# Low one-hots from the read banks on ScalarE instead of a compare on VectorE

## What is computed

```python
item_emb = concat(table_i1[item[:, 0]], table_i2[item[:, 1]], table_i3[item[:, 2]])        # 96 wide
ub = concat(table_i1[rec_his[:, :, 0]], table_i2[rec_his[:, :, 1]], table_i3[rec_his[:, :, 2]])
h = concat(q, ub, q - ub, q * ub) @ w_att1.T + b_att1       # q: item_emb at each position
score = (h @ w_att2.T + b_att2)[..., 0]                     # linear in ub, given q
score = where(rec_his[:, :, 0] == 0, 0.0, score)
browse = einsum('bl,ble->be', score, ub)
x = dice(concat(item_emb, browse, user_emb) @ w1.T + b1)
x = dice(x @ w2.T + b2)
out = sigmoid(x @ w3.T + b3)
```

## Time and profile before

| | |
|---|---|
| three timed runs | 1511.55, 1507.39, 1504.20 us |
| span of the profiled execution | 1506.3 us (its time outside the span is not given) |
| VectorE, TensorE, GpSimd, ScalarE busy | 93%, 86%, 79%, 50% |
| mean TensorE clock granted | 0.957 of full |
| main loop | about 50 to 1450 us |

### The profile page before, as it was taken

The page is one execution under the profiler, slowest core; times in us unless marked ns, Lnnn a source line. Parts: engine busy times, 40 slices in busy tenths (PEclk is TensorE's granted clock), DMA queues, the critical chain, the costliest instruction groups (busy, mean ns, idle before and its releaser), DMA issues.

```text
span 1506.3 us, 66273 instructions
## 1 busy us (share of the span) xinstructions
PE 1299.2 (86%) x27007; PEld 1186.0 (79%) x27007; DVE 1405.9 (93%) x1397; ACT 758.1 (50%) x1729; POOL 1188.4 (79%) x1671
## 2 busy tenths in 40 slices
PE   5688989889898988889898998989899898988864
PEld 4577878888887988788788888878888887888761
DVE  6699999999999999899999999999999999999945
ACT  5554455555445555454555554454555545452217
POOL 3588788888888888788888888888888888888830
PEclk8899999999999999999999999999999999999966
DMA  3566676666667666666766666666676666565820
GB/s 51 111 137 127 127 143 133 141 144 141 124 137 143 130 146 140 127 133 133 143 131 142 146 141 134 130 137 132 143 143 140 141 132 138 131 149 133 153 54 1
DMA packets 517508, 194.38 MB, mean 129 GB/s; under 512 B 485445, under 2 KB 493237, under 8 KB 517245
## 3 DMA queue, kind: packets, MB, share of 16 engines
q1 hardware_dynamic: 499654, 162.61, 53.5%
q10 hardware_dynamic: 15448, 26.51, 6.7%
q0 software_dynamic: 2144, 1.36, 0.8%
HBM read 8.45 MB, written 1.44 MB: 7 GB/s over the span
## 4 chain that ended last, share of the span: by engine, by line
POOL 72%; issue 15%; PE 3%; DVE 3%; POOLq 3%; ACT 2%; DMA 1%; ACTq 1%; SPq 0%; DVEq 0%
POOL score L439 24%; POOL score_r L448 14%; POOL score L444 11%; POOL parts L449 9%; POOL parts L452 6%; POOL item_rows L417 4%; POOL parts L445 3%; POOL user_rows L425 2%; DVE score_j L1026 1%; DVE onehot_lo L1012 1%; ACT scores_b L775 1%; PE sel L727 1%; DMA hiT<-onehot_hi 1%; POOLq L437 1%; POOLq L443 1%
## 5 line engine op out<-in xcount | busy, mean ns | idle before, releaser
L560 PE MATMUL wsum_ps<-scaled_lo,onehot_hi 100*128 100x75 bf16 x12288 | 535.0, 201 | 81.5 <-DVE scaled_lo L1038 80.2
L543 PEld LDWEIGHTS sel<-scoretab,hiT 128*128 128x128 bf16 x12288 | 495.8, 99 | 121.6 <-DMA hiT<-onehot_hi 59.2
L543 PE MATMUL sel<-scoretab,hiT 128*128 128x75 bf16 x12288 | 534.5, 201 | 63.1 <-DMA hiT<-onehot_hi 43.9
L1038 DVE TENSOR_TENSOR scaled_lo<-onehot_lo,parts 100x3744 bf16<-100x3744 bf16 x256 | 539.0, 2105 | 34.4 <-POOL parts L452 26.4
L560 PEld LDWEIGHTS wsum_ps<-scaled_lo,onehot_hi 100*128 100x128 bf16 x12288 | 486.1, 99 | 106.3 <-DVE scaled_lo L1038 101.7
L439 POOL TENSOR_TENSOR score<-score_j 100x16 f32<-100x16 f32 x256 | 386.6, 1510 | 156.6 <-DVE score_j L1026 155.7
L768 ACT ACTIVATE wsum_ring<-wsum_ps 128x300 f32<-128x300 f32 x512 | 215.5, 421 | 525.7 <-PE wsum_ps L560 497.2
L1026 DVE TENSOR_REDUCE score_j<-sel 100x24 f32<-100x600 f32 x512 | 395.5, 772 | 21.0 <-PE sel L543 21.0
L994 DVE TENSOR_TENSOR onehot_hi<-digits,iota_hi 100x1920 bf16<-100x1920 bf16 x256 | 296.1, 1157 | 3.4 <-PE wsum_ps L560 3.3
L775 ACT ACTIVATE scores_b<-acc 128x512 bf16<-128x512 f32 (+1 forms) x318 | 255.4, 803 | 50.0 <-issue 22.7
L448 POOL TENSOR_TENSOR score_r<-score,parts 100x16 f32<-100x16 f32 x256 | 207.3, 810 | 20.0
(11 more groups left out here) (168 smaller groups left out, 724.0 us busy)
## 6 DMA issues: line engine op xcount, KB each, us to landing
scoretab<-scores_b SPq DMA_DIRECT2D x384, 93.8 KB
weightsum<-wsum_ring ACTq DMA_DIRECT2D x128, 125.0 KB
weightsum<-wsum_ring ACTq DMA_DIRECT2D x64, 150.0 KB
raw<-in_r_rec_his_dram SPq DMA_DIRECT2D x32, 150.0 KB
hiT<-onehot_hi SPq DMA_TRANSPOSE x256, 3.8
x_rows<-x_tile SPq DMA_DIRECT2D x14, 100.0 KB
scores_b<-x_rows SPq DMA_DIRECT2D x1, 1400.0 KB
item_rows<-in_L_rec_table_i_dram,ids_now POOLq DMA_INDIRECT x51
```

Source lines behind the costliest of these rows:

```text
L543: mm = pe.matmul(sel[:, 2 * (s % 2) + q, (c % 4) * W:(c % 4 + 1) * W] .rearrange("p (j v) -> p j v", j=NF), hiT[0:HJ, s // 2 % 4, g * POSP ...
L560: mm = pe.matmul(wsum_ps[:, s % 2, b * W:(b + 1) * W].rearrange("p (j v) -> p j v", j=NF), hi_columns(ring_slot(n), g), scaled_lo[:, n % 2 ...
L1038: ins = dve.tensor_tensor(scaled_lo[:, n % 2, :, :, :].rearrange("p q i (u d) -> p (q i) u d", d=2), onehot_lo[:, n % 2, :, :, :].rearrang ...
```

## The change

The low compare on VectorE goes. ScalarE makes the low one-hots, 8 half histories at a time, out of the banks that `read_scores` filled: `relu(1 + x / 2^100)` is 1 in the matching column and 0 in all others. It does so after VectorE's pick of the same slot and behind `copy_sums` in its own order; `read_scores` two slots later waits for it too. `onehot_lo` has four buffers instead of two and no padding column in each feature (76 columns a half history instead of 78). The rim rows are centred and squared once, in the digit task, into `rims`; `lo_rows` copies them in one activation instead of two, and in each even slot it stands behind the low one-hots.

```diff
+    LOWS = 4
-        onehot_lo = sb("onehot_lo", [POS, 2, PER, NF, LP], BF16)
+        onehot_lo = sb("onehot_lo", [POS, LOWS, PER, U], BF16)
...
                     pe.wait_ge(score_ready, k - 1)
+                    pe.wait_ge(lo_ready, k - 1)
...
-                    ins = act.activation(digits[:, hb, kind, :, :, :].rearrange("p g j d -> p j g d"),
...
+                    else:
+                        rims_j = rims[:, hb, :, :, :].rearrange("p g j i -> p j g i")
+                        act.activation(rims_j[:, :, :, 0], src, ACT.Identity, bias=centre[:, :])
+                        ins = act.activation(rims_j[:, :, :, 1], src, ACT.Square, bias=centre[:, :])
...
-                act.activation(rows[:, :, :, 0], low, ACT.Identity, bias=centre[:, :])
-                act.activation(rows[:, :, :, 1], low, ACT.Square, bias=centre[:, :]).then_inc(lo_rows_ready, 1)
+                act.activation(onehot_hi[0:POS, ring_slot(n), :, 1:1 + 2 * NF],
+                               rims[:, hb, g0:g0 + PER, :, :].rearrange("p g j i -> p g (j i)"), ACT.Copy
+                               ).then_inc(lo_rows_ready, 1)
+
+            def onehot_low(t, s):
+
+                k = t * SLOTS + s
+                n, g0 = s // 2, (s % 2) * 8
+                if s % 2 == 0 and not (isinstance(k, int) and k < 2 * LOWS):
+                    act.wait_ge(scaled_ready, t * STEPS + n - LOWS + 1)
+                act.wait_ge(score_ready, k + 1)
+                act.activation(onehot_lo[:, n % LOWS, g0:g0 + 8, 0:W].rearrange("p (q c) u -> p q c u", q=2),
+                               sel[0:POS, 2 * (s % 2):2 * (s % 2) + 2, 0:4 * W].rearrange("p q (c u) -> p q c u", u=W),
+                               ACT.Relu, bias=one[:, :], scale=1.0 / FAR).then_inc(lo_ready, 1)
...
                     copy_sums(t - 1, s - LAG + SLOTS)
+                onehot_low(t, s)
...
-            def onehot_low(t, n):
...
-                dve.wait_ge(lo_ready, k + 1)
+                dve.wait_ge(lo_ready, 2 * k + 2)
...
-                onehot_low(t, n)
```

More of the change, by code:

```diff
@@ L35, in build @@
     HB = 8
-    LP = LO + 1
-    HJ, U, W = HB + NF * HI, NF * LP, NF * LO
+    HJ, W = HB + NF * HI, NF * LO
+    U = W + 1
     TILE, HALF = 128, 64
@@ L77, in build @@
         parts = sb("parts", [POS, 2, PER, 3, 2], BF16)
-        digits = sb("digits", [POS, 2, 2, 2 * HALF, NF, 2], BF16)
+        digits = sb("digits", [POS, 2, 2 * HALF, NF, 2], BF16)
+        rims = sb("rims", [POS, 2, 2 * HALF, NF, 2], BF16)
         far_rows = sb("far_rows", [1, 3, LO], BF16)
@@ L94, in build @@
         iota_hi = sb("iota_hi", [POS, HI], BF16)
-        iota_lo = sb("iota_lo", [POS, LP], BF16)
+        iota_lo = sb("iota_lo", [POS, LO], BF16)
+        one = sb("one", [POS, 1])
         identf = sb("identf", [128, 128])
@@ L478, in _ @@
             chain(pool.tensor_copy(iota_hi[:, :], iota_i[:, :]))
-            chain(pool.iota(iota_i[:, 0:LP], pattern=[[1, LP]], base=-LO, channel_multiplier=0))
-            chain(pool.tensor_copy(iota_lo[:, :], iota_i[:, 0:LP]))
+            chain(pool.iota(iota_i[:, 0:LO], pattern=[[1, LO]], base=-LO, channel_multiplier=0))
+            chain(pool.tensor_copy(iota_lo[:, :], iota_i[:, 0:LO]))
             column = far_column[:, :]
@@ L921, in slot @@
                     split_copy(r, stage, SPLIT_DONE * (t + 1) + (3 * r + stage + 1), 1 - odd)
-            act.wait_ge(bias_ready, 4)
+            act.wait_ge(bias_ready, 6)
             scale_raw(0, 0)
@@ L994, in onehot_high @@
                 dve.tensor_tensor(onehot_hi[0:POS, ring_slot(n), :, HB:].rearrange("p g (j v d) -> p g j v d", j=NF, d=2),
-                                  digits[:, hb, 1, g0:g0 + PER, :, :].unsqueeze(3)
+                                  digits[:, hb, g0:g0 + PER, :, :].unsqueeze(3)
                                   .to_broadcast([POS, PER, NF, HI // 2, 2]),
@@ L999, in onehot_high @@
                                   ALU.is_equal).then_inc(hi_ready, 1)
-            def onehot_low(t, n):
-                k = t * STEPS + n
-                hb, g0 = n // 8, (n % 8) * PER
-                if n == 0:
-                    dve.wait_ge(task_copied, DIGITS0 if isinstance(t, int) and t == 0 else tasks_start(t))
-                elif n == 8:
-                    dve.wait_ge(task_copied, task_before(t, 3) + 1)
-                if not (isinstance(k, int) and k < 2):
-                    dve.wait_ge(scaled_ready, k - 1)
-                dve.tensor_tensor(onehot_lo[:, n % 2, :, :, :].rearrange("p q j (v d) -> p (q j) v d", d=2),
-                                  digits[:, hb, 0, g0:g0 + PER, :, :].rearrange("p g j d -> p (g j) d").unsqueeze(2)
-                                  .to_broadcast([POS, PER * NF, LP // 2, 2]),
-                                  iota_lo[:, :].rearrange("p (v d) -> p v d", d=2).unsqueeze(1)
-                                  .to_broadcast([POS, PER * NF, LP // 2, 2]),
-                                  ALU.is_equal).then_inc(lo_ready, 1)
             def pick(t, s):
@@ L1076, in _ @@
             dve.memset(offset[:, :], -float(MID) / LO).then_inc(bias_ready, 1)
+            dve.memset(one[:, :], 1.0).then_inc(bias_ready, 1)
+            dve.memset(onehot_lo[:, :, :, W:U], 0.0).then_inc(bias_ready, 1)
             dve.memset(w2col[:, :], 0.0).then_inc(dve_tail_pre, 1)
```

15 lines of the change are left out of this document (7 added, 8 removed).

## The result

The changed kernel is slower: median 1530.4 us of 4 runs (1524.9 to 1534.2), against 1506.5 us (1504.2 to 1511.6) for the kernel before in the same jobs. The ratio is 1.016, 95% interval 1.013 to 1.018. Forecast were 1440 us and a range of 1380 to 1494, so the kernel went the other way, and the time lies outside the range.

What follows compares the result with a forecast made beforehand. VectorE was taken to set the step. Stretches summed to 80.7 us a tile, 83.4 with coupling, minus 3.8; 15 tiles gave -57, the last -8, taking 1506.3 to about 1440 us, range 1380 to 1494.

Steps and rivals of the forecast that it cites:

- VectorE, bare step 4.44 us: VectorE's step without a wait: 5.24 us less 0.80 for the dropped low compare and the shorter scale.
- GpSimd, 0.1 us a step and gather steps of 5.47: GpSimd loses the compare's cover, charged 0.1 us a step; its chain sets steps 3 to 5 at 5.47 each.
- ScalarE, low at 0.79 us: Each new ScalarE activation making low one-hots from 100x600 of PSUM takes 0.79 us, bounds 0.56 and 0.95 after overlap.
- Digit task, "two 384-element activations, about 0.5 each against 0.86: plus 0.15": ScalarE's digit task for low becomes two activations instead of one copy, adding 0.15 us, twice a tile.
- TensorE, 17.1 us computed for steps 6 to 8 "so 16.0 after": TensorE's work there is 17.1 us; running up to a slot ahead, it would leave 16.0, against 16.20 before.
- The new coupling: Two longer loops over the engines cost 0.25 us in each of 11 steps: 2.7 us a tile, bounds 0 and 7.
- Loop (a): Pick, low one-hots, split copy, split matmuls, read, next pick: 4.3 us and three handovers against VectorE's 4.54; just closes.
- Last tile, "about -8": With no split and no gathers, steps without a finish part go from 5.24 to 4.54 us, about -8 in all.
- the one that ended slower: Rival: late rim rows make transposes and reads late; at 3.3 us of lateness a tile is 91.0, 1560 us; chance 0.13.
- loop (b): The rim copy waits behind low one-hots, delaying SP's transpose and the read: 8.6 of two steps' 9.1 us.
- ScalarE takes it all back: Rival: low one-hots at 0.95 us, or coupling of 6 us a tile, give 1490 to 1512 us; chance 0.14.
- "Wrong, if": Four signs: low at 0.95; ScalarE idling on picks while TensorE awaits split copies; TensorE awaiting transposes; TensorE's clock dropping more.

Runs made afterwards that it cites:

- e5: The changed kernel with contiguous rims activations and the low one-hots moved to the end of each ScalarE slot: 1437.0 us, 0.953 of the kernel before.
- e1: The changed kernel with rims in two planes, so each rims activation writes one contiguous run: 1493.4 us, 0.991 of the kernel before.
- e7: e5 with SP's transpose issued ahead of the three score transfers in a tile's last two steps: 1446.0 us, 0.962 of the kernel before.
- e9: e1 with ScalarE's third group of sums transfers moved from slots 28 to 30 to slots 0 to 2 of the next tile: 1470.7 us, 0.978.
- e12: e1 with the low one-hots behind the rim copy and its row transfers but ahead of the split copies: 1479.6 us, 0.981 of the kernel before.
- e13: e1 with the split copies first, then the low one-hots, then the rim copy and its row transfers: 1475.4 us, 0.982 of the kernel before.

## Why the prediction was wrong

Step by step:

- *VectorE, bare step 4.44 us*: right. 4.47 us in a step without a wait (step 14), of which the changed kernel's timeline shows these three operations:

```profile
847.59 1.20 DVE L1013 TENSOR_TENSOR onehot_hi<-digits,iota_hi 100x1920 bf16<-100x1920 bf16 x1
848.72 0.77 DVE L1027 TENSOR_REDUCE score_j<-sel 100x24 f32<-100x600 f32 x1
849.41 2.04 DVE L1039 TENSOR_TENSOR scaled_lo<-onehot_lo,parts 100x3648 bf16<-100x3648 bf16 x1
```

- *GpSimd, 0.1 us a step and gather steps of 5.47*: right in size. VectorE waited 7.0 us for it in the changed kernel and 24.6 in e5; gather steps took 5.4 to 5.6 us where nothing else was late.
- *ScalarE, low at 0.79 us*: right, 0.761. *Rim copy about 0.25*: 0.285, also right. *Digit task, "two 384-element activations, about 0.5 each against 0.86: plus 0.15"*: **the first step that failed.** They took 1.55 and 1.71 us. From the first one's start to their successor's it is 2.45 us, against 1.0 forecast, 32 times 1.45 = 46 us of ScalarE, always in the same two slots of a tile. The price came from a slope over rows in which the output is written in one run or in pairs that fill a word; that these write every sixth half was in the code and not in the sum. e1, near the price of the forecast (0.57 and 0.59), is 37 us faster.
- *TensorE, 17.1 us computed for steps 6 to 8 "so 16.0 after"*: the computed 17.1 was right (17.2 in the changed kernel and e1). The lead of a slot that was to hide 1.1 us of it did not. Probably, with every step shorter, there is no longer a slack stretch ahead in which to build it; where the least else was late some of it came back (16.8 in e5, 16.4 in e7).
- *The new coupling, "2.7 us a tile, bounds 0 and 7"*: **the second step that failed, and the larger one.** In e1 ScalarE's work is what was forecast, 62.2 us in the tile of the middle (the sum of its windows):

```profile
sum 87.34, PE 79.83 PEld 74.75 DVE 73.67 ACT 62.21 POOL 62.16; mean PE 15.97 PEld 14.95 DVE 14.73 ACT 12.44 POOL 12.43
```

  Yet its mean tile takes 87.6 us, 6.9 above the 80.7 without coupling. The 6.9 are a remainder and not all coupling: by stretch they are +1.0, +1.0, +1.2, -0.9 and +4.6, and the +1.2 is TensorE's own work in steps 6 to 8. What the place of low costs is measured by e5: moving it behind the rest takes 4.3 us off e1's tile, where 2.7 were forecast, and 3.1 of them in steps 12 to 15. There the forecast had its largest gain ("VectorE's 21.52 busy less 4 x 0.80 plus some GpSimd waits, 18.5") and in the sum of that stretch no wait for transposed one-hots; e1 took 23.1, and 2.5 of that went with three sums transfers (e9). So the queue of ScalarE was named as the danger, but its price was too small and its worst place, the seam, was priced as VectorE's alone.

  Loop (a) did not close even by its own terms. 0.77 + 0.79 + 0.80 + 0.97 + 1.01 is 4.34 us, and with three handovers of 0.1 it is 4.6 against the 4.54 of a step. The forecast also closed each loop with every other engine on time ("It just closes"), and noted that a sums DMA or a digit task beside it breaks it; with split copies in 21 of 32 slots, sums transfers in 12 and four digit tasks a tile that is the normal case. The two loops share the queue, so relieving one leaves the other (e12, e13). With low last the tile is 83.3 us, 2.6 above 80.7. That this equals the forecast's 2.7, and the 1437 its 1440, is partly luck: the stretches miss by -1.2 to +1.5.
- *Last tile, "about -8"*: its first 15 steps took 79.6 us against 82.2, minus 2.6. A third, smaller miss; why is not shown.

Two of the forecast's sums are off by 0.1 us (4.5 + 5.3 + 4.7 - 0.3 is 14.2, TensorE's terms add up to 74.4), and nothing hangs on it. The two errors in bold and TensorE's 1.2 make up most of the miss in the tile; the rest of the 6.9, which low last doesn't take away either, is not split further. 80.7 + 6.9 is e1's tile, and 2.5 more for the rims is the changed kernel's 90.1, where 83.4 was forecast. Over tiles 1 to 14 the 4.2 us by which the 6.9 exceed the forecast's 2.7 are 59 us, the rims' 2.5 are 35 (37 between the medians of e1 and the changed kernel). Against the kernel before, 14 tiles of 2.46 us more are 34 us; first and last tile, prologue and tail give 8 back, and 26 is what the span grew by.

Of the rivals, the one that ended slower named loop (b) alone and put its price at 1560; its loop is real, but freed alone it gives back 14 us. "ScalarE takes it all back" allowed a coupling of 6 us a tile and would have been the result had the rims cost what was said: e1 took 1493 us, in its span of 1490 to 1512 (its other condition, low at 0.95 us, did not come). The rule quoted there from the Trainium skill, that a relu belongs on VectorE, does not decide this case: e5 has the relu on ScalarE and runs in 0.953 of the time before. Two of the four signs at the end of the forecast ("Wrong, if") are what the new trace shows: ScalarE idling on picks (53 us) while TensorE waits for split copies, and the falling clock.

## What to carry to other kernels

Price a moved operation by the shape of what it writes, not by its element count: a strided store of half-words took nearly three times the contiguous one. When work goes onto an engine whose queue runs in order, list what stands behind it and who waits for that, and put it behind everything that someone waits for sooner; here the place in the slot was worth 43 to 56 us, and the whole change at its best 68. A loop of several engines that "just closes" in a forecast should be counted as open: here each of the others was late at times too. And a stretch where transfers crowd is to be priced by who waits for them, not by the busiest engine alone.

## What the runs showed of the hardware

- ScalarE, 384 elements out of fp32 PSUM with a bias operand: 0.57 to 0.59 us written as contiguous bf16, 0.95 us as fp32 at 24-byte steps, 1.55 (Identity) and 1.71 us (Square) as bf16 at 12-byte steps. The old pair copy writes 768 bf16 elements as adjacent pairs at the same steps in 0.85 us. Contiguous rows of the same two functions are cheap, and so are whole words at the same 12-byte steps: what costs most is a half-word that stands alone in its word. The Trainium skill (ScalarE: Activation LUTs, What ACT_TABLE_LOAD costs) gives 280 ns plus 0.833 ns an element for an activation with such a bias: by it 0.60 us for 384 elements and 0.78 for low's 600. The contiguous rims and low (0.76) agree; the ones with gaps take 2.6 and 2.8 times that. The Trainium skill (SBUF — State Buffer, Door 1: The DMA port swizzle) has lines of 16 bytes in SBUF, and a price for each access that crosses into a new one. By it the fp32 layout, with a new line for every element, should be the dearest; it is not, so that rule alone does not explain the rows, and the cause stays open.
- The gaps are far cheaper on the reading side: e1's rim copy, which gathers 96 elements out of the contiguous buffer, took 0.37 us instead of 0.285.
- TensorE pays twice for a wait: behind idle times of 1.74 and 1.92 us in the changed kernel and of 5.56 us in e1 its granted clock fell to 0.50, and the next read of 24 matmuls took 1.71, 1.60 and 1.70 us instead of 1.0.
